# Second layer of a two-layer cross-attention kernel: on VectorE, PM of the next head stands before ZP of this one, not behind it

## The reference

```python
q = heads(hidden_states @ W_q); k_t = heads(text_ehs @ W_k); v_t = heads(text_ehs @ W_v)
probs_t = jax.nn.softmax(einsum('bhsd,bhtd->bhst', q, k_t) * attn_scale, axis=-1)
text_out = einsum('bhst,bhtd->bhsd', probs_t, v_t)
attn_scores = einsum('bhsd,bhnd->bhsn', q, heads(ip_ehs @ W_k_ip)) * attn_scale
qsem = _l2norm(einsum('bhst,bte->bhse', probs_t, text_ehs))
sem = einsum('bhse,bne->bhsn', qsem, _l2norm(ip_ehs))
probs_ip = softmax(attn_scores + SEM_SCALE * sem, axis=-1) * spatial_mask
ip_out = einsum('bhsn,bhnd->bhsd', probs_ip, v_ip)
out = (text_out + ip_out) @ W_out + b_out + residual
```

## Time and profile before

| | |
|---|---|
| median of 3 runs | 1632.13 us (1630.63 to 1632.45) |
| profiled execution | 1630.7 us, its span 1628.7 us |
| PE busy | 96% of the span |
| DVE busy | 86% |
| ACT busy | 62% |
| POOL busy | 44% |
| granted TensorE clock, mean | 0.982 |

### The profile page before, as it was taken

How to read it: one execution, slowest core, us unless ns; L and a number is a source line. 1 busy time by engine, 2 the same in 40 slices (tenths; PEclk the granted TensorE clock), 3 DMA queues, 4 the chain that set the end, 5 groups by cost and what they waited for, 6 DMA issues and landing times. The chain is left out here.

```text
span 1628.7 us, 42423 instructions
## 1 busy us (share of the span) xinstructions
PE 1560.4 (96%) x13960; PEld 1385.5 (85%) x13960; DVE 1393.6 (86%) x4083; ACT 1015.7 (62%) x2444; POOL 717.3 (44%) x629
## 2 busy tenths in 40 slices
PE   6999999999999999998999999999999999999986
PEld 5888888888888888777798888988898889898876
DVE  4687787877888888876899999999999999999995
ACT  3455556566565655655667767667676776676652
POOL 3234432223322322433556655655555565565442
PEclk9999999999999999998999999999999999999998
DMA  8334444444444444443324323332333233332311
GB/s 228 99 107 118 123 128 131 119 125 129 122 127 125 117 127 125 135 123 109 88 82 123 102 76 111 106 101 72 104 104 105 75 103 96 104 99 71 94 38 36
DMA packets 204098, 175.29 MB, mean 108 GB/s; under 512 B 45312, under 2 KB 203402, under 8 KB 203882
## 3 DMA queue, kind: packets, MB, share of 16 engines
q1 hardware_dynamic: 203882, 172.59, 36.8%
HBM read 112.12 MB, written 60.38 MB: 106 GB/s over the span
## 5 line engine op out<-in xcount | busy, mean ns | idle before, releaser
L1061 POOL TENSOR_TENSOR ZS<-ZP 128x256 f32<-128x256 f32 x267 | 275.4, 1032 | 279.7 <-DVE ZP L968 279.7
L616 ACT ACTIVATE P<-TA 128x512 f32<-128x512 f32 x320 | 202.3, 632 | 278.4 <-DVE TA L956 275.2
L336 PE MATMUL NAT<-KS,QS 65*128 65x256 f32 x1280 | 299.2, 316 | 7.6 <-ACT SC L570 5.5
L978 DVE SCALAR_TENSOR_TENSOR PM<-P,PH 128x512 f32<-128x512 f32 x320 | 275.2, 860 | 0.0
L350 PE MATMUL TR<-QS,KS 69*128 69x256 f32 (+2 forms) x1280 | 258.7, 284 | 4.3 <-DVE TA L956 2.1
L144 PE MATMUL GP<-PH,GH 128*128 128x256 f32 x936 | 241.7, 288 | 17.6 <-DVE ZP L968 17.3
L336 PEld LDWEIGHTS NAT<-KS,QS 65*128 65x128 f32 x1280 | 201.1, 192 | 63.3 <-issue 48.4
L863 DVE TENSOR_REDUCE MX<-NAT 128x2 f32<-128x504 f32 x320 | 215.8, 675 | 34.6 <-PE NAT L336 31.1
L284 POOL TENSOR_TENSOR PARTS<-QKF,PARTS 112x512 fp32r<-112x512 f32 (+1 forms) x93 | 121.5, 1307 | 278.4 <-ACT PARTS L646 233.3
L144 PE MATMUL GP<-PH,GL 128*128 128x256 f32 x936 | 236.3, 281 | 0.0
L619 ACT ACTIVATE P<-TR 128x512 f32<-128x512 f32 x320 | 193.0, 603 | 59.0 <-PE TR L350 58.2
(11 more groups left out here) (269 smaller groups left out, 3817.4 us busy)
## 6 DMA issues: line engine op xcount, KB each, us to landing
QS<-qk_parts SPq DMA_DIRECT2D x480, 64.0 KB
KS<-qk_parts SPq DMA_DIRECT2D x480, 64.0 KB
qk_parts<-PARTS SPq DMA_DIRECT2D x128, 224.0 KB, 2.9
CT<-in_ctx_t SPq DMA_DIRECT2D x32, 512.0 KB, 3.9
qk_parts<-PARTS SPq DMA_DIRECT2D x64, 192.0 KB, 2.4
XT<-in_x_t SPq DMA_DIRECT2D x48, 112.0 KB, 2.6
XT<-x_t SPq DMA_DIRECT2D x48, 112.0 KB, 2.4
XB<-in_x SPq DMA_DIRECT2D x16, 320.0 KB, 4.0
```

The costliest lines, as they stand in the source:

```text
L336: ins = e.matmul(NAT[s % 2][:, i * T:(i + 1) * T], QS[0:KQ, h, i * 128:(i + 1) * 128], KS[0:KQ, h, :], start=True, stop=True)
L616: e.activation(P[:, s % NP, :], TA[:, s % 2, :], ACT.Exp, scale=SCALE).then_inc(q["exp"], 1)
L978: e.scalar_tensor_tensor(PM[:, s % 2, :], P[:, (S1 + s) % NP, :], 2.0, PH[:, s % NS, :].bitcast(F32), ALU.mult, ALU.subtract).then_inc(q[" ...
L1061: e.tensor_tensor(ZS[s % NZ][:, :], ZP[:, s % 2, 0:S], ZP[:, s % 2, S:2 * S], ALU.add).then_inc(q["zs"], 1)
```

## The change

In the DVE program the block of PM is moved from behind ZP and the root step to a place before ZP. Both blocks are otherwise as they were, with all their waits. Since lines move, ZP has line 975 and PM line 967 in the kernel after.

```diff
@@ -959,6 +959,13 @@
                     e.wait_ge(q["tail"], s - S1 + 3)
                     ins = e.memset(TR[s % 2][96:128, S:2 * S], 0.0)
                 ins.then_inc(q["sum"], 1)
+            s = t - 1 - S1
+            if 0 <= s < S1:
+                if s >= 2:
+                    e.wait_ge(q["zp"], s - 1)
+                e.wait_ge(q["ph"], s + 1)
+                e.scalar_tensor_tensor(PM[:, s % 2, :], P[:, (S1 + s) % NP, :], 2.0, PH[:, s % NS, :].bitcast(F32), ALU.mult,
+                                       ALU.subtract).then_inc(q["pm"], 1)
             s = t - 2 - S1
             if 0 <= s < S1:
                 if s >= 2:
@@ -970,13 +977,6 @@
                 b = at1(t, "rs", 1, n)
                 if b is not None:
                     root_step(e, b, 2 * n + 1)
-            s = t - 1 - S1
-            if 0 <= s < S1:
-                if s >= 2:
-                    e.wait_ge(q["zp"], s - 1)
-                e.wait_ge(q["ph"], s + 1)
-                e.scalar_tensor_tensor(PM[:, s % 2, :], P[:, (S1 + s) % NP, :], 2.0, PH[:, s % NS, :].bitcast(F32), ALU.mult,
-                                       ALU.subtract).then_inc(q["pm"], 1)
             b = of0(t, AT0["num"])
             if b is not None:
                 if b:
```

## The result

| | before | after |
|---|---|---|
| median | 1631.38 us (1626.64 to 1632.45, 4 runs) | 1687.51 us (1683.85 to 1688.48, 4 runs) |
| profiled execution | 1630.7 us, span 1628.7 | 1688.48 us, span 1686.7 |

The change makes the kernel slower by 3.5%: ratio 1.0351, 95% interval 1.0333 to 1.0368. The forecast was 1686 us.

What follows compares the result with a forecast made beforehand. PE and DVE were both taken as nearly full, so their handovers count. Terms of 0.6 + 0.9 + 1.2 + 0.9 + 0 + 0.1 = 3.7 us a batch, 15 x 3.6 = 54 us, gave 1686 us; range 1660 to 1710 (0.64).

Steps and rivals of the forecast that it cites:

- Term 1: Slot with HTL and no other product on PE, where PE already waits: ZP and GP +0.60 us a batch.
- Term 2: Four slots with little spare time between ZP and GP: +0.9 us a batch together, ends 0.4 and 1.2.
- Term 3: Long POOL instructions stall PM, now before ZP: CTSL +1.2 us, third PARTS +0.9, first two PARTS 0 a batch.
- The race at the first two PARTS: Whether PM or PARTS starts first in those two slots: -0.2 to +1.4 us for both, taken as 0.
- all races are lost: Rival: PARTS comes ahead of PM and other terms reach upper ends; 6.1 us a batch, 1724 us; chance 0.13.
- Term 4: After ZP, POOL's ZS gets in ahead of PM and delays it: +0.1 us a batch, ends 0 and 1.0.
- What would show it: Signs in the trace: PE's wait for ZP 13.4 to about 65 us, PM about 2 us at CTSL, ZS about 740 ns.
- The count: Whole kernel: 3.7 us a batch summed, then 15 batches at 3.6 us, 54 us in all.
- only the order: Rival: PM's stalls fall elsewhere, only the later ZP costs; 1.0 to 1.8 us a batch, 1647 to 1659; chance 0.15.
- Faster: Rival: DVE is what the batch waits for, 57 us of stalls could go; -14 us, 1618; chance 0.04.

Runs made afterwards that it cites:

- POOL's short work: Against the kernel before, order kept: POOL's PARTS, CTSL, XTSL and VIP of the second layer work on 64 columns only; 1627.78 us, 0.9984.
- heads 0 and 4: Against the kernel before: PM before ZP only in the two slots of the first and second PARTS; 1623.73 us, 0.9970.

## Why the prediction was right

*Term 1* (0.60 us at the slot where PE waits): measured 0.60 us in the trace, and 12 us by the kernel that does this alone, for 9 forecast. At equal clock that kernel lost 8 to 9 us, which is the term.

*Term 2* (0.9 us for four places) named the four slots (lines 917, 939, 278, 825 are those of heads 19, 3, 11, 12), and at the last the wrong cause: line 825 stands before MX there and not behind it, and it is the MN that XTSL stalls. A fifth place, head 7, was missing: from ZP's end to GP it had 0.54 us, no more than head 11's 0.56. All five together cost 18 us, 1.2 us a batch, the upper end of the range that I gave for four.

*Term 3*: CTSL 1.2 us a batch forecast, 16 us in 15 batches measured; CTSL and the third PARTS together 2.1 forecast, 34 us measured, 2.3 a batch. The race at the first two PARTS came out as rows 9 pointed: PM is first, and this brings 0.3% of the kernel. I had put that at up to 0.2 us a batch; it is 0.3. A lost race would have been the rival "all races are lost".

*Term 4* (ZS ahead of PM): ZS did fall to 744 ns, so the first place did change hands. PM itself lost little, as forecast; what I missed is that the small MN of line 884 is stalled in the same way. In the groups between 800 and 1560 us its mean is 383 ns after, and 231 before:

```profile
L884 DVE SCALAR_TENSOR_TENSOR MN<-MX,MN 128x8 fp32r<-128x8 f32 x66 | 25.3, 383 | 0.0
```

*What would show it*: PE's wait for ZP was to grow to about 65 us and grew to 43.5. The mechanism holds, but this row undercounts it. A product that follows a wait is recorded longer (0.36 us for 0.28), and PE's busy time in a batch rises from 52.20 to 53.35 us for the same 482 products:

```profile
1150.01:1207.21 57.20, 53.35 (x482) 47.54 (x481) 50.34 (x107) 37.09 (x97) 24.76 (x29) 1.00 0.32 90
```

That is 1.15 us a batch, 16 us in the 14 batches of these 800 us. The other signs came: DVE's wait for GP 1.5 us, its wait for NAT 81.5, a PM of 2.24 us at CTSL with GP 1.09 us late behind it, ZS 744 ns, PE's busy share 94%.

*The count*: 57.20 - 52.99 = 4.2 us a batch where I had 3.7. The span grew by 58.0 us, which is 13.8 such batches and not 15; the first and the last batches lose less. The two errors cancel in part, which is why 1686 came nearer to 1687.5 than the terms deserve: that nearness is luck.

*The clock* had no term in the sum. Its mean is 0.982 in the profiled execution of before and 0.976 to 0.980 in the four runs of after. What such a difference is worth shows in the kernel before itself: 17 runs of it on one chip go from 1625.7 us at 0.986 to 1633.2 us at 0.981. From that I estimate that some 5 us of the 56 go with the clock. In the trace of after the windows 1033 to 1037 and 1262 to 1266 us have 0.57, with PE at 1.2 GHz for part of them; before has 1.00 in each window of 100 us from 860 to 1460 us. In the 7 us before the second of these falls PE was busy for 5.65 us, but in the same place one batch earlier it was busy for 5.64 and the clock stayed at 1.00. That PE's new idle time brings the clock down is therefore likely and not shown.

*The rivals*: "only the order" gives 28 us, half of the loss. "Faster" rested on 57 us of stalled DVE time; 56 us of it went with POOL's short work and brought 2 us, 40 us of it went with heads 0 and 4 (320 x (860 - 735) ns) and brought 5. In both kernels PE still stood for ZP in the slot of head 15.

## What to carry to other kernels

Ask of each instruction in an engine's row who waits for it. An instruction that nobody waits for belongs behind the one that the bounding engine waits for; here PM then was also the one that POOL's long instructions held up, at almost no cost. In two slots, where ZP was not ready yet and a long POOL operation was about to start, the same move was a small gain (0.3%): decide by slot, not for the loop.

## What the runs showed of the hardware

DVE's single-input MN (line 871, a tensor_scalar) was held up by ZS as well, 0.40 us for 0.16, while ZP, with an input in PSUM, and the reduction MX never were: over all the traces the longest ZP took 694 ns and the longest MX 685, for means of 676 and 675. After PARTS, POOL's ZS was let in ahead of a PM that had stood for 0.8 us. After CTSL the PM ended first, and the ZS that stood directly behind CTSL on POOL took 1.20 us for 0.73. Why, no run here tells.
